# Rows added on GpSimd and norms on ScalarE in a single-head attention stage

## The reference, cut to what matters

```python
x = x + tanh(g_ffn[0]) * ffn0(layernorm(x), ...)          # four expert rows for each token
x = x + tanh(g_xattn[1]) * L1_xattn(layernorm(x), ctx, ctx, W1, b1, W2, b2, gamma, beta)
```

```text
X   = X + sum of the four rows of the experts           (already weighted and gated)
hn  = (X - mean) / sqrt(var + 1e-5)
p   = softmax(hn @ ctx^T / 16);  y = p @ ctx + hn
xn  = (y - mean) / sqrt(var + 1e-6);  x1 = xn * gamma + beta
o   = relu(x1 @ W1 + b1) @ W2 + b2 + x1
X   = X + gate * (gamma * (o - mean) / sqrt(var + 1e-6) + beta)
```

## Time and profile before

| what | value |
|---|---|
| three runs | 1762.08, 1763.86, 1765.33 us |
| the profiled execution | 1762.41 us |
| its span | 1760.6 us, 38383 instructions |
| mean granted TensorE clock | 0.992 of full |
| busy: TensorE, weight load | 1662.8 us (94%), 1301.1 us (74%) |
| busy: VectorE, ScalarE, GpSimd | 1132.2 us (64%), 984.9 us (56%), 940.0 us (53%) |
| DMA | 140.28 MB, mean 80 GB/s |
| the stage's first addition on TensorE | 364.80 us |
| the next stage's first fetch of weights | 484.02 us |

### The profile page before, as it was taken

The page is one execution under the profiler, slowest core; times in us unless marked ns, Lnnn a source line. Parts: engine busy times, 40 slices in busy tenths (PEclk is TensorE's granted clock), DMA queues, the critical chain, the costliest instruction groups (busy, mean ns, idle before and its releaser), DMA issues. The chain is left out here.

```text
span 1760.6 us, 38383 instructions
## 1 busy us (share of the span) xinstructions
PE 1662.8 (94%) x11883; PEld 1301.1 (74%) x11928; DVE 1132.2 (64%) x3349; ACT 984.9 (56%) x2789; POOL 940.0 (53%) x1138
## 2 busy tenths in 40 slices
PE   7999799989789999999999999989998999989998
PEld 4777478858646777777777777768876888867886
DVE  4787666638656666766667676547886353337875
ACT  4677445524435566665666656547772355536775
POOL 2366675535446655665555655333677244447752
PEclk9999899999999999999999999999999999999999
DMA  4333276565020000000000000012445344432200
GB/s 155 96 103 117 98 234 196 165 209 180 21 107 4 6 4 4 4 5 5 4 4 4 5 5 4 5 49 79 148 145 183 94 128 146 134 133 77 76 26 25
DMA packets 79670, 140.28 MB, mean 80 GB/s; under 512 B 11729, under 2 KB 61105, under 8 KB 77297
## 3 DMA queue, kind: packets, MB, share of 16 engines
q1 hardware_dynamic: 65744, 98.22, 17.9%
q0 software_dynamic: 13728, 39.60, 6.4%
HBM read 84.88 MB, written 50.82 MB: 77 GB/s over the span
## 5 line engine op out<-in xcount | busy, mean ns | idle before, releaser
L1545 POOL TENSOR_TENSOR L1f_rn<-L1f_ss,L1f_root_c 128x8 f32<-128x8 f32 x64 | 105.9, 1655 | 183.1 <-DVE L1f_ss L1848 181.4
L1681 PE MATMUL L1f_psQ<-L1f_xT,arena 128*128 128x128 f32 x1408 | 172.4, 275 | 0.9 <-ACT L1f_xT L1756 0.9
L1681 PEld LDWEIGHTS L1f_psQ<-L1f_xT,arena 128*128 128x128 f32 x1408 | 169.5, 192 | 4.4 <-ACT L1f_xT L1756 1.1
L1774 ACT ACTIVATE L1f_sg<-L1f_psQ,vec1f 128x128 f32<-128x128 f32 x192 | 63.5, 364 | 137.2 <-PE L1f_psQ L1681 137.1
L2073 POOL DMA_INDIRECT outs_L2f<-L2f_tiles_ys,L2f_tiles_spot x79 | 76.0, 962 | 119.1 <-ACT L2f_tiles_ys L2218 110.0
L1560 POOL TENSOR_TENSOR L1f_rot<-L1f_qn,L1f_sinT 128x512 f32<-128x512 f32 x64 | 113.4, 1792 | 28.8 <-DVE L1f_qn L1864 28.8
L1894 DVE SCALAR_TENSOR_TENSOR L1f_hid<-L1f_psQ,vec1f,L1f_sg 128x128 f32<-128x128 f32 x192 | 61.4, 346 | 92.1 <-ACT L1f_sg L1774 91.9
L1605 PE MATMUL L1f_psQ<-arena,L1f_hT 128*128 128x512 f32 x256 | 118.4, 605 | 0.6 <-ACT L1f_hT L1763 0.6
L2073 POOL DMA_INDIRECT outs_L0f<-L0f_tiles_ys,L0f_tiles_spot x79 | 76.0, 962 | 48.0 <-ACT L0f_tiles_ys L2218 42.7
L1693 PE MATMUL L1f_psB<-arena,L1f_hid 128*128 128x256 f32 (+1 forms) x384 | 99.8, 388 | 0.0
L1550 POOL TENSOR_TENSOR L1f_pr<-L1f_pr,L1f_rs 128x512 f32<-128x512 f32 x64 | 95.6, 1515 | 6.2 <-DVE L1f_rs L1858 6.2
(11 more groups left out here) (533 smaller groups left out, 4642.6 us busy)
## 6 DMA issues: line engine op xcount, KB each, us to landing
L0f_tiles_xs<-rows_L0f SPq DMA_DIRECT2D x79, 144.0 KB, 2.4
L2f_tiles_xs<-rows_L2f SPq DMA_DIRECT2D x79, 144.0 KB, 2.3
arena<-in_w_L2f SPq DMA_DIRECT2D x8, 1120.0 KB, 6.2
arena<-in_w_L1f SPq DMA_DIRECT2D x8, 1088.0 KB, 7.5
L1x_got<-outs_L0f SPq DMA_DIRECT2D x16, 512.0 KB, 4.0
L3x_got<-outs_L2f SPq DMA_DIRECT2D x16, 512.0 KB, 3.4
arena<-in_w_L0f SPq DMA_DIRECT2D x8, 768.0 KB, 4.9
rows_L0f<-zero SPq DMA_DIRECT2D x31, 144.0 KB, 2.7
```

The source lines that it names most:

```text
L1545: nc.gpsimd.tensor_tensor(rn[:, s.p, h], ss[:, s.p, h], root_c[:, 0:LH], ALU.pow).then_inc(s_rn, 1)
L1681: mm = nc.tensor.matmul(out, w, xT[:, k], start=(k == 0), stop=(k == KC - 1), skip_group_check=True)
L1774: nc.scalar.activation(sg[to, u], unit_out(u, 0, of), ACT.Gelu, bias=column(s, 2 * KC + u)[of]).then_inc(s_sg, 1)
```

## The change

- Rows: for sequences 2 to 15, GpSimd adds row 1 to row 0 of the fetched four (`pairs`, one operation of 128x256, ahead of all else in its round), and TensorE sums rows 0, 2 and 3. Sequences 0 and 1 are summed as before.
- Order on TensorE: `combine` now opens the round, ahead of `turn_weights`; `turn_in` stands ahead of `values`.
- Norms: both `rows` and `centre` of VectorE become ScalarE activations (`norm` and `centre`), at the head of ScalarE's round. GpSimd makes the bias column -mean * rstd for each, a third operation in `root1` and in `root2`.
- VectorE: the order becomes add, attended, tops, update, last_stats. `attended` also waits until the xn of two sequences before has been made.

```diff
+        ALL_BY_PE = 2
@@ gpsimd
             def root1(s):
-                own = slice(s.n, s.n + 1)
-                pool.wait_ge(s_mv1, s.n + 1)
-                inverse_root(c.var[:, own], c.rstd[:, own], c.mv[:, s.n, 1:2], 1e-5, s_r1, 2 * s.n)
+                root(nc, pool, c, s, s_mv1, s_r1, 1e-5)
+
+            def pairs(s):
+                if s.n >= ALL_BY_PE:
+                    pool.wait_ge(s_got[s.n % 3], 16 * (s.n // 3) + 16)
+                    nc.gpsimd.tensor_tensor(got[:, s.n % 3, 0], got[:, s.n % 3, 0], got[:, s.n % 3, 1], ALU.add).then_inc(s_pair, 1)
 
             def root2(s):
...
-                inverse_root(v2[:, own], r2[:, own], mv2[:, s.p, 1:2], 1e-6, s_r2, 2 * s.n)
+                inverse_root(v2[:, own], r2[:, own], mv2[:, s.p, 1:2], 1e-6, s_r2, 3 * s.n)
+                pool.wait_ge(s_r2, 3 * s.n + 2)
+                nc.gpsimd.tensor_scalar(n2[:, own], mv2[:, s.p, 0:1], r2[:, own], -1.0, ALU.mult, ALU.mult).then_inc(s_r2, 1)
...
-            each_round([(beta_rows, 1), (root1, 2), (root2, -1), (root3, -3)], LOW, HIGH)
+            each_round([(pairs, 3), (beta_rows, 1), (root1, 2), (root2, -1), (root3, -3)], LOW, HIGH)
@@ tensor
             def combine(s):
                 pe.wait_ge(s_got[s.n % 3], 16 * (s.n // 3) + 16)
                 after(pe, s_x, s.n)
+                after(pe, s_pair, s.n + 1 - ALL_BY_PE)
                 for j in range(TOPK):
+                    if j == 1 and s.n >= ALL_BY_PE:
+                        continue
...
-            each_round([(turn_weights, -1), (combine, 2), (turn_rows, -2), (values, -1), (turn_in, 1), (scores, 0), (hidden, -2),
+            each_round([(combine, 2), (turn_weights, -1), (turn_rows, -2), (turn_in, 1), (values, -1), (scores, 0), (hidden, -2),
                         (output, -3)], LOW, HIGH)
@@ scalar
+            def norm(s):
+                act.wait_ge(s_r1, 3 * s.n + 3)
+                after(act, s_T, s.n - 2)
+                nc.scalar.activation(hn[:, s.n % 3], c.X[:, s.n], ACT.Identity, scale=c.rstd[:, s.n:s.n + 1],
+                                     bias=c.tmp[:, s.n:s.n + 1]).then_inc(s_hn, 1)
+
+            def centre(s):
+                act.wait_ge(s_r2, 3 * s.n + 3)
+                after(act, s_T2, s.n - 1)
+                nc.scalar.activation(xn[:, s.p], y[:, s.p], ACT.Identity, scale=r2[:, s.p:s.p + 1],
+                                     bias=n2[:, s.p:s.p + 1]).then_inc(s_xn, 1)
...
-            each_round([(turned, -1), (affine, -2), (rows, 1), (exps, 0), (hidden, -2)], LOW, HIGH)
+            each_round([(centre, -2), (norm, 1), (turned, -1), (affine, -2), (rows, 1), (exps, 0), (hidden, -2)], LOW, HIGH)
@@ vector
-            def rows(s):
-                dve.wait_ge(s_r1, 2 * s.n + 2)
-                after(dve, s_T, s.n - 2)
-                shifted(hn[:, s.n % 3], c.X[:, s.n], c.mv[:, s.n], c.rstd[:, s.n:s.n + 1]).then_inc(s_hn, 1)
...
                 dve.wait_ge(s_hn, s.n + 1)
+                after(dve, s_xn, s.n - 1)
...
-            def centre(s):
-                dve.wait_ge(s_r2, 2 * s.n + 2)
-                after(dve, s_T2, s.n - 1)
-                shifted(xn[:, s.p], y[:, s.p], mv2[:, s.p], r2[:, s.p:s.p + 1]).then_inc(s_xn, 1)
...
-            each_round([(centre, -2), (rows, 1), (update, -4), (add, 2), (attended, -1), (tops, 0), (last_stats, -3)], LOW, HIGH + 1)
+            each_round([(add, 2), (attended, -1), (tops, 0), (update, -4), (last_stats, -3)], LOW, HIGH + 1)
```

More of the change, by code:

```diff
@@ L1192, in single_attention @@
         mv2, mv3 = ph.sb("mv2", [P, 2, 2]), ph.sb("mv3", [P, 2, 2])
-        v2, r2, v3, r3, rg = (ph.sb(n, [P, 2]) for n in ("v2", "r2", "v3", "r3", "rg"))
+        v2, r2, n2, v3, r3, rg = (ph.sb(n, [P, 2]) for n in ("v2", "r2", "n2", "v3", "r3", "rg"))
         gb, bb = ph.sb("gb", [P, D]), ph.sb("bb", [P, KC])
@@ L1198, in single_attention @@
         (s_gb, s_g, s_x, s_st1, s_mv1, s_r1, s_hn, s_xb, s_T, s_hT, s_S, s_mx, s_exp, s_pt, s_pT, s_v, s_rs, s_y, s_st2, s_mv2,
-         s_r2, s_xn, s_T2, s_x1, s_x1b, s_H, s_h1, s_o, s_st3, s_mv3, s_r3, s_t, s_out) = ph.semaphores(
-            "gb g x st1 mv1 r1 hn xb T hT S mx exp pt pT v rs y st2 mv2 r2 xn T2 x1 x1b H h1 o st3 mv3 r3 t out")
+         s_r2, s_xn, s_T2, s_x1, s_x1b, s_H, s_h1, s_o, s_st3, s_mv3, s_r3, s_t, s_out, s_pair) = ph.semaphores(
+            "gb g x st1 mv1 r1 hn xb T hT S mx exp pt pT v rs y st2 mv2 r2 xn T2 x1 x1b H h1 o st3 mv3 r3 t out pair")
         block = ph.block()
         LOW, HIGH = -4, NB + 4
+        ALL_BY_PE = 2
         @block.sync
@@ L1374, in _ @@
             c.wait(dve, "L1x")
-            def shifted(dst, src, mv, root):
-                return nc.vector.tensor_scalar(dst, src, mv[:, 0:1], root, ALU.subtract, ALU.mult)
             def add(s):
```

## The result

The changed kernel took 1756.88 us in the median of six runs (1754.21 to 1758.32), the kernel before 1765.59 (1762.08 to 1769.69). The ratio is 0.9949, 95% interval [0.9934, 0.9964], so 6 to 12 us less. The forecast was 1754.6 us, 9.3 less than the 1763.86 known then; the two medians here lie 8.7 apart.

The account below looks back on a forecast made before the run. Hand-overs between nearly full TensorE and VectorE were taken to bound the single attention's round at 6.09 us. Ten rounds -7.8, fill -1.0 and drain -0.5 gave -9.3: 1763.86 to 1754.6 us, own range 1751.0 to 1758, with B to 1761.

Parts of the forecast that it names:

- The loop before: Single attention's full rounds: one path through TensorE and VectorE hand-overs takes 12.17 us in two rounds, 6.09 a round.
- TensorE alone 5.48 with four rows: TensorE's full round without waits while it adds four rows: 5.48 us; afterwards, with three rows, 5.05.
- VectorE bounds nothing any more, update at 0.48: VectorE's round falls to 4.5 us without norms, the update behind the maxima taking 0.48 us for 0.88.
- Rival B: GpSimd's two additions are each held 0.48 us by VectorE on shared SBUF ports: 5.79 a round, 1759.4 us, chance 0.16.
- The prediction's argument from L1381: Against B: VectorE's y reads one source from PSUM, as L1381 does, which kept to 0.41 to 0.43 us in all sixteen.
- GpSimd alone 5.1: GpSimd's round without a wait, three roots of 1.24 and two additions of 0.70: 5.1 us, making it the fullest engine.
- the new loop 5.31: Two-round loop from root3 through all of GpSimd, ScalarE's norms, TensorE and VectorE's statistics: 10.63 us, 5.31 a round.
- Gain 0.78 a round: Full rounds of the single attention fall from 6.09 to 5.31 us, 7.8 us in ten rounds.
- Fill, -1.0: First rounds: later hn against additions moved into the first exponential's wait, slow clock kept; -1.0 us, between +2 and -2.5.
- Drain, -0.5 (0 to -1.2): Last two to three rounds: TensorE waits less for xn because ScalarE's norm follows its root directly; -0.5 us.
- The sum, -9.3: Whole kernel: -7.8 in full rounds, -1.0 fill, -0.5 drain, giving 1754.6 us from the 1763.86 median.
- Rivals C and D: C: waits for GpSimd undo the gain, 1762.9 us, chance 0.10; D: TensorE's clock stays low behind the fill, 1769, chance 0.08.

Follow-up runs that it names:

- the reordering: Changed kernel with GpSimd's beta row addition behind root2 instead of ahead of root1: period 5.38 us, stage 109.8 us, ratio 0.9944 to the kernel before.

## Why the prediction was right, and where it was off

- *The loop before*, 12.17 in two rounds: right. Taking the update and its wait out of it, and nothing else, gave the forecast TensorE-bound round.
- *TensorE alone 5.48 with four rows*: 5.42, measured without idle time.
- *VectorE bounds nothing any more, update at 0.48*: right; 0.48 in sixteen of sixteen. Rival B did not come about, since GpSimd's two additions end before the update starts. GpSimd's small roots run beside it and cost it nothing. The prediction's argument from L1381 against B was empty, since in a full round before that addition ran beside none of GpSimd's (434.05 to 434.46, GpSimd's beta row 432.67 to 433.40). What it was to show holds: y, with one source in PSUM, runs beside the beta row in nine rounds after, and neither is longer (0.48 from 429.41, 0.73 from 429.33).
- *GpSimd alone 5.1, the new loop 5.31*: the mis-sized term. GpSimd alone is 5.38, each root 0.07 longer than the 1.24 of the earlier trace rows where the next piece is another root, and the beta row 0.83 with the hand-over behind it instead of 0.70. The loop contains all of GpSimd, so it grew as well: from root3 to the end of root2 5.29 us for 5.13, the rest 5.47 for 5.50, together 10.76 for 10.63. That left GpSimd's queue and the loop both at 5.38, and the reordering showed that the queue sets the period even where the loop is shorter. The period came out 0.07 off, inside the 5.1 to 5.8 that the prediction set as the test of its loop; that test could not tell the two bounds apart, and that they lie so close is luck.
- *Gain 0.78 a round*: 0.71. The prediction gave no shares to the parts, and its text suggests that the work taken off mattered. It hardly did: the update's place alone gives 0.67, and the other three parts add 0.04 to it in the full rounds. The prediction credited the move with 0.40, the delay of the update; what it is worth is that the update, its statistics and its wait (1.55 us in two rounds) leave the loop. The pairs (5.55 without them), and the two norms (5.42 without) are each worth little, since every one of them leads to a bound near 5.4. What the rest of the change brought, 4.2 us of the stage, lies mostly in the emptying (3.3, of which 0.5 is a shorter dip), then in the fill (0.6) and ten rounds (0.3).
- *Fill, -1.0*: -2.3. The prediction kept the dip of before; without it the fill gained 0.9, so the reasoning was right in size. That the dip was missing can't be put down to the change with certainty, since it was missing with the update moved alone too.
- *Drain, -0.5 (0 to -1.2)*: a second mis-sized term. It came to -1.2, with a dip of 1.7 us inside that nobody had forecast; without it -2.8. TensorE's waits for xn in the last rounds, 1.48 and 1.58 before, are 0.50 and 1.19 after, and the gain falls on four rounds (0.5, 1.0, 1.0, 0.4) and not two to three.
- *The sum, -9.3*: the stage gained 10.4. The full rounds gave 0.9 less than forecast, and the two dips, one that went and one that came, nearly cancel (-1.4 and +1.7). That the total lies as close as it does is partly luck.
- *Rivals C and D*: did not occur. With the update first the changed kernel's rounds are longer than before (6.43 for 6.09), by another mechanism than C's or D's.

## What to carry to other kernels

In a pipeline of in-order queues, first lay out the loop that sets the round and ask which of its pieces nobody downstream is waiting for: moving such a piece behind the one that the other engine needs can give nearly everything that offloading gives. An engine that only takes work over has to be summed from start to start of its dependent small operations, not from their busy times, before one calls it free; here a third operation of 0.26 us takes 0.35 from start to start, and without one of the two the round was 0.26 shorter, until VectorE's loop bound. A change that leaves the full rounds alone can still move the filling and the emptying by microseconds each way, so read the three apart, between marks that stand at the same place of the round. And compare a stage between its own marks when total times scatter by more than the effect.

## What was not expected of the hardware

TensorE's clock fell at the stage's end. In the changed kernel the last hidden layer came after idle times of 1.19 and 0.90 us and took 1.86 us in the first profile (1.99 in the second); before, after idle times of 1.58 and 0.90, it took 1.16. The granted clock from 465 to 468 us was 0.64 of full (2.4 GHz), so part of the stretch ran at the lower level, 1.2 GHz:

```profile
464.23 0.44 PE L1312 MATMUL L1x_psX<-consts,L1x_xn 128*128 128x128 f32 x2 [1.19 <-ACT L1x_xn L1357]
465.56 1.86 PE L1320 MATMUL L1x_psH<-L1x_x1T,arena 128*128 128x128 f32 x8 [0.90 <-ACT L1x_x1T L1376]
```

```profile
465.00:468.00 3.00, 2.44 (x10) 2.33 (x11) 0.91 (x2) 1.75 (x6) 0.09 (x1) 0.64 0.02 5
```

It cost 1.7 us there (4.13 from this row to the end of the output, 2.47 before). It is not tied to the change: the kernel with the update moved alone showed it (2.08), and the changed kernel with the beta row moved did not (1.16). Of the eleven profiles that leave these waits empty, six show it and five don't (before, both norms on VectorE, update first, beta row moved, weights first). With matmuls put into both waits it did not fall:

```profile
455.61 0.44 PE L1314 MATMUL L1x_psX<-consts,L1x_xn 128*128 128x128 f32 x2
456.95 1.16 PE L1324 MATMUL L1x_psH<-L1x_x1T,arena 128*128 128x128 f32 x8 [0.25 <-ACT L1x_x1T L1374]
```

That is one profile against six with and five without the dip, so it doesn't show that the filled waits prevent it.

VectorE beside GpSimd: the update of two SBUF sources was 0.88 beside additions of 128x256 and 0.48 beside GpSimd's operations of one column, which also read SBUF. The Trainium skill, "SBUF — State Buffer", section "SBUF: two separate sides", has the lock for any GpSimd operation that reads SBUF; here only the large ones showed.
